# Gate logits from columns of the value blocks and from transposed normalised rows, and rows stored in four pieces, in a two-layer gated cross-attention kernel

## The reference

```python
x = x + tanh(g_xattn[0]) * L0_xattn(layernorm(x), ctx)
x = x + tanh(g_ffn[0]) * L0_ffn(layernorm(x))        # quantised gate/up/down
x = x + tanh(g_xattn[1]) * L1_xattn(layernorm(x), ctx)   # 16 heads, relative bias
x = x + tanh(g_ffn[1]) * L1_ffn(layernorm(x))        # 8 experts, the best one only
```

```python
x_red = x @ w_red                                    # 256 -> 16
logits = x_red @ (wg / norm(wg)).T                   # 16 -> 8
gates = softmax(logits); scores = max(gates); idx = argmax(gates)
h = gelu(x @ W1[idx] + b1[idx]); o = (h @ W2[idx] + b2[idx]) * scores
```

## Time and profile before

| | us |
|---|---|
| median of 3 runs | 456.87 (456.45 to 460.0) |
| profiled execution | 460.95 |
| its span, first to last instruction | 459.2 |
| TensorE busy | 405.7 (88%) |
| VectorE busy | 323.5 (70%) |
| ScalarE busy | 251.1 (55%) |
| POOL busy | 128.7 (28%) |
| mean granted TensorE clock | 0.958 |

### The profile page before, as it was taken

One profiled execution on the slowest core, in us unless ns is written; L12 is line 12 of the kernel. 1 busy time (PEld: TensorE's weight loads), 2 busy tenths in 40 slices (PEclk: granted clock), 3 DMA queues, 4 the chain that ended last, 5 costly groups with the idle time before them and its releaser, 6 DMA issues.

```text
span 459.2 us, 7477 instructions
## 1 busy us (share of the span) xinstructions
PE 405.7 (88%) x2436; PEld 289.4 (63%) x2437; DVE 323.5 (70%) x661; ACT 251.1 (55%) x420; POOL 128.7 (28%) x144
## 2 busy tenths in 40 slices
PE   7998899999996039999999999999958799999993
PEld 7877644444443038878877767876746476767762
DVE  4999984369998998964777898775473365555652
ACT  3564655579998965512487767777423323424210
POOL 6523155000000350421195000100126345351222
PEclk9999999999999558999999999999997899999998
DMA  8910000000001013000399000000092212121000
GB/s 244 287 5 0 1 3 0 0 0 0 0 1 61 1 38 73 1 0 0 127 396 390 7 1 2 0 1 2 10 267 77 64 55 66 52 60 33 27 21 1
DMA packets 27424, 27.25 MB, mean 59 GB/s; under 512 B 11611, under 2 KB 23586, under 8 KB 27139
## 3 DMA queue, kind: packets, MB, share of 16 engines
q1 hardware_dynamic: 25187, 21.73, 15.3%
q0 software_dynamic: 2208, 5.14, 3.9%
HBM read 22.63 MB, written 5.15 MB: 61 GB/s over the span
## 4 chain that ended last, share of the span: by engine, by line
PE 57%; DVE 21%; issue 4%; DMA 3%; ACT 2%; POOL 1%; DVEq 0%; POOLq 0%; ACTq 0%
PE quad L1668 24%; PE bank L1668 23%; PE bank L1961 4%; DVE amP L1371 3%; DVE big_g L1402 2%; PE bank L2156 2%; DMA token_rows<-x_rows 2%; DVE mx L1498 2%; DVE big_g L486 2%; DVE big_g L1499 2%; PE quad L1712 1%; DVE big_g L1496 1%; DVE amZ L1305 1%; DVE amU L1311 1%; PE bank L1712 1%
## 5 line engine op out<-in xcount | busy, mean ns | idle before, releaser
L1668 PE MATMUL quad<-yT,ffn_w 128*128 (+1 forms) x128 | 56.3, 593 | 0.0
L1668 PE MATMUL quad<-big_g,yT 128*128 x92 | 43.3, 613 | 3.5 <-issue 3.5
L769 ACT ACTIVATE big_u<-bank 77x512 f32<-77x512 f32 (+2 forms) x72 | 39.0, 593 | 11.2 <-PE bank L1961 10.4
L1067 ACT ACTIVATE yT<-yT 128x512 f32<-128x512 f32 x23 | 14.5, 630 | 53.0 <-DVE yT L1623 53.0
L1668 PEld LDWEIGHTS quad<-yT,ffn_w 128*128 128x128 f32 x128 | 24.0, 190 | 29.5 <-issue 28.3
L1668 PE MATMUL bank<-big_u,yT 128*128 x184 | 41.8, 380 | 0.2 <-DVE yT L1637 0.2
L746 POOL DMA_INDIRECT out<-yT,k_blockdiag x23 | 23.4, 1015 | 55.3 <-DVE yT L1637 48.4
L1668 PEld LDWEIGHTS bank<-big_u,yT 128*128 128x128 f32 x184 | 34.1, 190 | 5.0 <-issue 0.9
L1961 PE MATMUL bank<-ident,big_g 128*77 128x128 f32 x256 | 34.7, 278 | 1.2 <-ACT big_g L994 0.9
L1623 DVE TENSOR_TENSOR yT<-quad,ffn_w 128x512 f32<-128x512 f32 x23 | 15.9, 691 | 25.3 <-PE quad L1668 18.6
L1668 PE MATMUL quad<-ffn_w,big_u 128*128 128x256 f32 x144 | 31.6, 380 | 0.6 <-ACT big_u L769 0.6
(11 more groups left out here) (321 smaller groups left out, 913.5 us busy)
## 6 DMA issues: line engine op xcount, KB each, us to landing
big_g<-in_L_ffn_W SPq DMA_DIRECT2D x1, 4096.0 KB, 13.4
big_u<-in_L_ffn_W SPq DMA_DIRECT2D x1, 4096.0 KB, 24.9
x_rows<-in_x SPq DMA_DIRECT2D x4, 512.0 KB, 6.5
ffn_w<-in_L_ffn_b SPq DMA_DIRECT2D x1, 2048.0 KB, 26.8
tmp<-bias_by_distance SPq DMA_DIRECT2D x2, 616.0 KB, 6.8
token_rows<-x_rows SPq DMA_DIRECT2D x1, 1032.0 KB, 10.7
tmp<-in_L_ffn_b SPq DMA_DIRECT2D x1, 1024.0 KB, 6.4
token_rows<-x_rows SPq DMA_DIRECT2D x1, 774.0 KB, 11.9
```

The lines of the kernel that those rows point to most:

```text
L769: act.activation(out_, in_, ACT.Copy, **k).then_inc(done, 1)
L1067: act.activation(hb[:, u, :], hb[:, u, :], ACT.Gelu).then_inc(s.gelu_sb, 1)
L1668: return pe.matmul(out_, lhsT=lhsT, rhs=rhs, start=first, stop=last)
```

## The change

The logits of a finished row are those of the row before attention, plus those of the attended part and of the output bias. So they are now made in three parts, without the finished rows.

- Operand stage: the values transposed (`VT`), the output matrix transposed (`WOT`), `WOT` times `GM` (`WOB`, spread over the heads of a half), and from these 8 more columns for each head in the value block `V1`, where zeros were, with the bias of the output in the first head. `heads` is as large as before. TensorE does it in `layer1_operands` and `value_logits`, with 10 of the 14 idle products between its two steps.
- `head_out` divides the gate columns too, and `gate_sums` adds them over the heads into `LA`. `y3_logits` multiplies the transposed normalised rows by `GM` in the pairs 6 and 8; `y3_logits_back` returns them in the last pair; VectorE multiplies them by the deviation before attention (`stdp`, new on POOL) and adds `LA`.
- `y4_in`, `logits` and `logits_back` are gone, with ScalarE's copies for them.
- The last pair has its own order on TensorE, VectorE and ScalarE. `project` is now one call for each tile.
- The last two tiles' mean and variance come from a sum taken with the residual and from squares on ScalarE, after the one-hots.
- POOL writes the two extra columns of the rows. SyncE stores four pieces: tiles 0 to 7, 8 to 11, 12 and 13, 14 and 15, and loads `B2` after the first piece, once the logits are back.
- The weights' split is on VectorE after the index, the products of `SHARE` are after `inputs` of the second tiles.
- Two small loads (columns of the two biases) are new, and the near-bias loads wait for the gate columns (`VGS`).

(Indentation and blank lines are cut.)

```diff
 sp.wait_ge(s.kbd_sb, 1)
 sp.dma_start(B1, row(a["L1_ffn_b1"].rearrange("e h -> (e h)")).to_broadcast([P, E * HID])).then_inc(s.ld_b, 16)
-sp.wait_ge(s.x3_done, NT)
-sp.dma_start(B2, row(a["L1_ffn_b2"].rearrange("e h -> (e h)")).to_broadcast([P, E * D])).then_inc(s.ld_b, 16)
 rows_t = rows_d.rearrange("(t p) c -> p t c", p=P)
-sp.wait_ge(s.ln_row, 1)
-sp.dma_start(rows_t[:, 0:TB, :], X[:, 0:TB, :]).then_inc(s.row_stored, 16)
-sp.dma_start(rows_t[:, TB:LAST, :], X[:, TB:LAST, :]).then_inc(s.row_stored, 16)
-sp.wait_ge(s.ln_row, 2)
-sp.dma_start(rows_t[:, LAST:NT, :], X[:, LAST:NT, :]).then_inc(s.row_stored, 16)
+for n, (b, e) in enumerate(ROW_PARTS):
+    if n == 1:
+        sp.wait_ge(s.lg_ps, 1)
+        sp.dma_start(B2, row(a["L1_ffn_b2"].rearrange("e h -> (e h)")).to_broadcast([P, E * D])).then_inc(s.ld_b, 16)
+    sp.wait_ge(s.ln_row, n + 1)
+    sp.dma_start(rows_t[:, b:e, :], X[:, b:e, :]).then_inc(s.row_stored, 16)
...
-rstds_of(0, TB, s.mv_d, s.rstd_d, TB)
-rstds_of(TB, LAST, s.mv_d, s.rstd_d, LAST)
-pool.wait_ge(s.rstd_d, 2)
+def rows_ready(b, e, n):
+    pool.wait_ge(s.mv_d, n)
+    c.link(pool.tensor_scalar(ve4[:, b:e], mv4[:, b:e, 1], EPS, None, ALU.add))
+    c.link(pool.tensor_tensor(rstd4[:, b:e], ve4[:, b:e], mhalf[:, b:e], ALU.pow))
+    pool.tensor_copy(X[:, b:e, RSTD], rstd4[:, b:e])
+    c.link(pool.tensor_scalar(ve4[:, b:e], mv4[:, b:e, 0], -1.0, None, ALU.mult))
+    pool.tensor_tensor(X[:, b:e, NMR], ve4[:, b:e], rstd4[:, b:e], ALU.mult).then_inc(s.ln_row, 1)
+for b, e in ROW_PARTS[:-1]:
+    rows_ready(b, e, e)
...
+pool.tensor_scalar(nmean[:, :], xsum[:, :], -1.0 / D, None, ALU.mult).then_inc(s.nmean_sb, 1)
+pool.wait_ge(s.dev_sb, 2)
+c.link(pool.tensor_scalar(ve4[:, LAST:NT], xdev[:, :], 1.0 / D, EPS, ALU.mult, ALU.add))
+c.link(pool.tensor_tensor(rstd4[:, LAST:NT], ve4[:, LAST:NT], mhalf[:, LAST:NT], ALU.pow))
+pool.tensor_copy(X[:, LAST:NT, RSTD], rstd4[:, LAST:NT])
+pool.wait_ge(s.nmean_sb, 1)
+pool.tensor_tensor(X[:, LAST:NT, NMR], nmean[:, :], rstd4[:, LAST:NT], ALU.mult).then_inc(s.ln_row, 1)
 c.link(pool.tensor_copy(rstdp[:, LAST:NT], rstd4[:, LAST:NT]))
 pool.wait_ge(s.lx_sb, 1)
...
+copy(WOT, pb[3].rearrange("p (c n) -> p c n", c=CH), s.l1_ps, WOTS, s.woT_sb)
+copy(WGNT[:, :], pb[7][0:G, WOG_AT + CH * E:WOG_AT + CH * E + E], s.l1_ps, WGT_, s.wgT_sb)
 act.wait_ge(s.keepv_sb, 1)
 for b in range(NB):
     copy(V1[:, b * H:(b + 1) * H, 0:HD], pb[5][0:KEYS, b * D:(b + 1) * D].rearrange("p (n d) -> p n d", d=HD),
          s.l1_ps, V1S, s.v1_sb, scale=keepv[:, b:b + 1])
+copy(GM[:, :, 0:E], pb[7][:, 0:CH * E].rearrange("p (c e) -> p c e", c=CH), s.l1_ps, GMS, s.gm_sb)
+for ci in range(CH):
+    o = VT_AT + ci * NB * KEYS
+    act.activation(VT[:, ci, :], pb[7][:, o:o + NB * KEYS], ACT.Identity, bias=bv1c[:, ci:ci + 1]).then_inc(s.vT_sb, 1)
+for b in range(NB):
+    copy(V1[:, b * H:(b + 1) * H, HD + 1:HD + 1 + E],
+         pb[6][0:KEYS, D + b * H * E:D + (b + 1) * H * E].rearrange("p (n e) -> p n e", e=E),
+         s.l1_ps, VGS, s.v1_sb, scale=keepv[:, b:b + 1])
 def ints(o, n, k):
...
+        return
+    if t in NEAR_AT:
+        n = NEAR_AT.index(t)
+        copy(lT[:, 2 * n:2 * n + 2, :], pb[7][:, 0:2 * P].rearrange("p (b n) -> p b n", b=2),
+             s.lT_ps, 2 * n + 2, s.lT_sb)
     weightsT(t, 0, 0)
...
+weightsT(LAST, 0, 0)
+exponents(LAST, 1, 0)
+weightsT(LAST, 0, 1)
+exponents(LAST, 1, 1)
 weightsT(LAST, 1, 0)
+heads_out(LAST, 0)
 attended(LAST - 2)
 weightsT(LAST, 1, 1)
...
+act.wait_ge(s.nmean_sb, 1)
+act.wait_ge(s.x3_done, NT)
+for u in range(2):
+    act.activation(e_[:, u, 0:D], X[:, LAST + u, 0:D], ACT.Square, bias=nmean[:, u:u + 1],
+                   accum_out=xdev[:, u:u + 1]).then_inc(s.dev_sb, 1)
...
+dve.wait_ge(s.l1_ps, WOGS)
+dve.tensor_tensor(WOB, pb[7][:, WOG_AT:WOG_AT + CH * E].rearrange("p (c e) -> p c e", c=CH)
+                  .unsqueeze(2).to_broadcast([P, CH, 8, E]),
+                  headof[:, :].unsqueeze(1).unsqueeze(3).to_broadcast([P, CH, 8, E]),
+                  ALU.mult).then_inc(s.wob_sb, 1)
 dve.wait_ge(s.ar_sb, MP)
...
+    o = pb[5 + u][:, 0:H * VE].rearrange("p (h d) -> p h d", d=VE)
     c.link(dve.reciprocal(rd[:, u, :], o[:, :, HD]))
+    mark = c.mark(dve.tensor_tensor(GA[:, u, :, :], o[:, :, HD + 1:HD + 1 + E],
+                                    rd[:, u, :].unsqueeze(2).to_broadcast([P, H, E]), ALU.mult))
     dve.tensor_tensor(att[:, u, :].rearrange("p (h d) -> p h d", d=HD), o[:, :, 0:HD],
                       rd[:, u, :].unsqueeze(2).to_broadcast([P, H, HD]), ALU.mult).then_inc(s.att_sb, 1)
+    return mark
+def gate_sums(t, mark):
+    dve.wait_ge(s.dve_step, mark)
+    return dve.tensor_reduce(LA[:, t:t + 2, :], GA.rearrange("p u h e -> p u e h"), AX.X, ALU.add)
+def last_heads_out():
+    dve.wait_ge(s.o_ps, LAST + 2)
+    o = quad[:, 0:2, 0:H * VE].rearrange("p u (h d) -> p u h d", d=VE)
+    c.link(dve.reciprocal(rd[:, :, :], o[:, :, :, HD]))
+    mark = c.mark(dve.tensor_tensor(GA, o[:, :, :, HD + 1:HD + 1 + E],
+                                    rd[:, :, :].unsqueeze(3).to_broadcast([P, 2, H, E]), ALU.mult))
+    dve.tensor_tensor(att.rearrange("p u (h d) -> p u h d", d=HD), o[:, :, :, 0:HD],
+                      rd[:, :, :].unsqueeze(3).to_broadcast([P, 2, H, HD]), ALU.mult).then_inc(s.att_sb, 2)
+    c.link(gate_sums(LAST, mark))
 def residual(t, u):
-    dve.wait_ge(s.wo_ps, t + 2)
-    x = X[:, tile_at(t) + u, 0:D]
-    dve.tensor_tensor(x, pb[5 if t == LAST else 4][:, u * D:(u + 1) * D], x, ALU.add).then_inc(s.x3_done, 1)
+    dve.wait_ge(s.wo_ps, t + (u if t == LAST else 1) + 1)
+    x, ps = X[:, tile_at(t) + u, 0:D], pb[5 - u if t == LAST else 4][:, u * D:(u + 1) * D]
+    if t == LAST:
+        ins = dve.scalar_tensor_tensor(x, ps, 1.0, x, ALU.mult, ALU.add, accum_out=xsum[:, u:u + 1])
+    else:
+        ins = dve.tensor_tensor(x, ps, x, ALU.add)
+    ins.then_inc(s.x3_done, 1)
...
+    if 4 <= t < LAST:
         dve.wait_ge(s.bo_added, 1)
         residual(t - 4, 0)
         residual(t - 4, 1)
         moments(t - 4)
     unit(t, 1, 0)
-    head_out(t - 2, 0)
+    if t < LAST:
+        head_out(t - 2, 0)
     unit(t, 1, 1)
-    head_out(t - 2, 1)
+    if t == LAST:
+        head_out(t - 2, 0)
+    c.mark(gate_sums(t - 2, head_out(t - 2, 1)))
 first_pair()
 for t in range(2, NT, 2):
     pair(t)
+residual(LAST - 4, 0)
+residual(LAST - 4, 1)
+moments(LAST - 4)
+dve.wait_ge(s.std_sb, 1)
+dve.wait_ge(s.lg_ps, 1)
+c.link(dve.tensor_tensor(LOG.rearrange("p (u b) e -> p u b e", u=4),
+                         pb[2].rearrange("p (b u x) -> p u b x", b=4, u=4)[:, :, :, 0:E],
+                         stdp[:, :].rearrange("p (u b) -> p u b", u=4).unsqueeze(3).to_broadcast([P, 4, 4, E]),
+                         ALU.mult))
 residual(LAST - 2, 0)
 residual(LAST - 2, 1)
 moments(LAST - 2)
-def ln_rows(a, b):
...
-dve.wait_ge(s.lg_ps, NT // 4)
-lg = pb[1].rearrange("p (t e) -> p t e", e=32)[:, :, 0:E]
+last_heads_out()
...
 dve.wait_ge(s.cnt_ps, 1)
...
-dve.wait_ge(s.vals_sb, 1)
+dve.wait_ge(s.ex_sb, 1)
+c.link(dve.tensor_reduce(coef[:, :], EX, AX.X, ALU.add))
+c.link(dve.reciprocal(coef[:, :], coef[:, :]))
+c.link(dve.tensor_scalar(coef[:, :], coef[:, :], tg[:, 3:4], None, ALU.mult))
+c.link(dve.tensor_copy(vals[:, :, 2], coef[:, :]))
...
-step(0, (0, 1), ())
+for u in range(2):
+    bias1(u, 0)
+shares()
+for u in range(2):
+    hidden(u, 0)
...
-    pe.transpose(pb[6][0:G, D:D + E], wgn[:, :], ident[0:E, 0:E]).then_inc(s.l1_ps, 1)
+    pe.transpose(pb[7][0:G, WOG_AT + CH * E:WOG_AT + CH * E + E], wgn[:, :], ident[0:E, 0:E]).then_inc(s.l1_ps, 1)
     pe.wait_ge(s.wgT_sb, 1)
     for ci in range(CH):
         ins = mm(pb[7][:, ci * E:(ci + 1) * E], WRT[:, ci * P:(ci + 1) * P], WGNT[:, :], True, True)
     ins.then_inc(s.l1_ps, 1)
+def value_logits():
+    pe.wait_ge(s.gm_sb, 1)
+    pe.wait_ge(s.woT_sb, 1)
+    pe.wait_ge(s.vT_sb, CH)
+    for rj in range(CH):
+        for ci in range(CH):
+            ins = mm(pb[7][:, WOG_AT + rj * E:WOG_AT + (rj + 1) * E], WOT[:, ci, rj * P:(rj + 1) * P],
+                     GM[:, ci, 0:E], ci == 0, ci == CH - 1)
+    ins.then_inc(s.l1_ps, 1)
+    idle_work(pb[3], 10)
+    pe.wait_ge(s.wob_sb, 1)
+    for b in range(NB):
+        for ci in reversed(range(CH)):
+            o = D + (b * H + ci * 8) * E
+            mm(pb[6][0:KEYS, o:o + 8 * E], VT[:, ci, b * KEYS:(b + 1) * KEYS],
+               WOB[:, ci, :, :].rearrange("p h e -> p (h e)"), True, ci > 0)
+        o = D + b * H * E
+        for ci in range(CH):
+            ins = mm(pb[6][0:KEYS, o:o + E], bo1c[:, ci:ci + 1].to_broadcast([P, KEYS]), GM[:, ci, 0:E],
+                     False, ci == CH - 1)
...
 pe.wait_ge(s.wT_sb, 9)
+value_logits()
 pe.wait_ge(s.p_done, NQB + 1)
-idle_work(pb[3], 14)
+idle_work(pb[3], 4)
...
     ins.then_inc(s.oT_ps, 1)
+def y3_logits(b):
+    for ci in range(CH):
+        for u in range(4):
+            o = (4 * u + b) * P
```

(55 more changed lines are left out.)

227 lines of the change are left out of this document (86 added, 141 removed).

## The result

| | before | after |
|---|---|---|
| median of 14 runs, us | 457.55 (456.45 to 460.62) | 454.43 (451.6 to 456.05, and one disturbed execution of 501.6) |
| profiled execution, us | 460.95 | 452.23 |
| its span, us | 459.2 | 450.5 |
| mean granted TensorE clock | 0.958 | 0.96 |

The ratio is 0.9917, with a 95% interval of 0.9895 to 0.9939: 0.8% faster, which counts as within 1%. Two later comparisons of the same two kernels gave 0.9946 (0.9919 to 0.9972) and 0.9935 (0.9909 to 0.996). The median fell by 3.1, 2.2 and 3.2 us. The median after is that of all 14 executions; without the disturbed one it is 454.18. The two profiled spans differ by 8.7 us, and most of the experiments ask what lies between 8.7 and 3.

What follows compares the result with a forecast made beforehand. TensorE bounds most stages, VectorE pairs 6 and 8, the last store the first gather. Span 459.2 + 3.0 + 1.3 - 6.4 + 0.6 = 457.7 us, shifted to the runs' median: 455.4 us; 8-in-10 range 450.8 to 459.5.

Steps and rivals of the forecast that it cites:

- Operand stage, +3.0 predicted: Before the pairs: new products delay `down` to 179.5 and the next stage to 200.6; +3.0 us, bounds +2.0 to +4.8.
- Pairs, +1.3 predicted: Attention pairs: VectorE's additions and TensorE's `y3_logits` show in near-bias pairs 6 and 8; +1.3 us, between 0.6 and 2.2.
- Gate, -6.4 predicted: Last pair to first gather: earlier index and stores start the gather at 339.6, not 345.99; -6.4 us, bounds -7.5 and -4.5.
- a slow clock as a rival: Operand stage: TensorE stays at 1.2 GHz until `down` runs, 4.8 + 2 us there, time 459.2; chance 0.05.
- decides, but only by 1.0 us: End of the gate before the change: the last store releases the first gather; without it the gather would wait for the index.
- the last store still decides: Rival at the gather: last piece takes 9.2 us, gather starts at 344.3, gain only 1.7, time 460.1; chance 0.08.
- Share products, +0.6 predicted: After the gather: share products move behind `inputs`, 1.14 us of TensorE, hidden only if the 2.94 us stand remains; +0.6 us.
- The stand of 2.94 us: First expert steps before the change: TensorE stands 2.94 us before 359.54, then runs at half its clock; no row explains it.
- the stand goes: Rival in the first expert steps: the 2.94 us stand and slow clock vanish, saving 4.7 us, time 451.2; chance 0.13.
- 453 to 458.5: The forecast's own range in us, from adding the bounds of the terms.
- signs named for "right": After-profile: `down` 3 to 4 us later, pairs 6 and 8 1 to 2 more, one-hots 5.7 earlier, gather 2.1 earlier, awaiting index.
- sign of "wrong": After-profile: gather released by `token_rows<-x_rows`; `down` before 177.5; pair without near bias over 12.35 us; bias waiting for share product.

Runs made afterwards that it cites:

- before_again: The kernel before, unchanged, profiled and timed again: median 457.03 us over 22 runs, profiled span 454.8 us.
- after_again: The changed kernel, unchanged, profiled and timed a second time: median 454.86 us over 10 runs, ratio to before 0.9946, profiled span 455.8 us.
- pair_sums_out: The changed kernel without VectorE's gate products and sums in pairs 0 to 12 (zeros instead): median 454.3 us over 10 runs.
- before_b2_early: The kernel before with one wait changed, so that B2 loads when the twelfth tile's rows are finished: one execution, 456.92 us.
- stores_undone: The changed kernel with the old transfer order, B2 loaded after the last residual and rows stored at the third and fourth signals: median 460.49 us.
- gate_columns_out: The changed kernel without the operands of the gate columns (zeros instead) and with 14 idle products as before: median 453.16 us over 7 runs.

## Why the prediction was right

Forecast 455.4, measured 454.4, 454.9 and 454.8; range 450.8 to 459.5; the chance of 0.72 was on within 1%. The call was right, and so was the main line of the mechanism: a gain of about 6 us in the gate, of which the stages ahead take a part back. That the sum came within 1 us is partly luck. The stages ahead were charged 4.3 us and take 1.8 to 2.8; against that, the half clock takes up to 1.5 us of the forecast gain in the gate and up to 2.8 us in layer 1 in some executions, and these were in no term of the sum. The profiles divide as follows, against before_again.

**Operand stage, +3.0 predicted: +1.0 or +2.0 at fill(0, 0), 1.7 in the time.** The order of the work came as predicted: idle products until 176.2, gate columns after, `down` at 178.5 to 179.5 with 179.5 forecast. Two sizes were off. The 16 records of the gate columns took 1.06 us with the clock up (176.18 to 177.25), 0.066 each, where I had taken 0.12 and 1.9 in all; they took 1.9 at the half clock in after_again, and 1.1 to 1.6 in the four other profiles with the late clock, which rose while they ran. And of the 3.4 us by which `down` starts later in after_again, 0.9 is gone at y3_in, mostly the wait for VectorE that TensorE no longer has, which was in the prediction, and another 0.6 at fill(0, 0), which was not; that VectorE, not delayed as much, is the bound of the second four tiles would explain it, but no run takes it apart.

**Pairs, +1.3 predicted: +0.8.** fill(6, 0) to fill(14, 0) is 52.3 us in all three profiles of the changed kernel, 51.5 before. It is VectorE's work as predicted, and pair_sums_out takes exactly this away. The step that failed is that TensorE's logits were charged ahead of `fill(8, 1)`, at 1.3 us a pair and 2.6 in the two: the 32 records of a pair took 1.06 us, and pair_sums_out, which keeps them and is back at the 13.44 us of before, shows that even those lie under VectorE.

**Gate, -6.4 predicted: -6.6 with the clock up, -4.9 to -5.1 with it down.** From fill(14, 0) to the gather: 39.67 us before, 33.08, 34.60 and 34.77 after. Counted from fill(14, 0), the one-hots are ready 0.6 us, the totals start 0.9 and the index is written 0.8 us earlier than forecast (340.37 less the 1.94 us by which fill(14, 0) is later is 338.4, for 339.25), since `token_back` came 0.7 earlier. What I did not see is written in the rows above: the new order lets TensorE stand 0.72, 1.51 and 0.75 us in a row. The waits were in my sum, their effect on the clock was not. I priced a slow clock as a rival only ahead of `down`.

**The store that "decides, but only by 1.0 us" was a misreading.** The gather starts 0.30 us after a store lands, but 0.93 us after VectorE has written the index (340.37 to 341.30). In the kernel before these two came out at 345.99 and 345.93: a tie. before_b2_early shows it. I took 0.3 for both. The 0.6 us that this lacks at the new start were covered by the path, which was 0.8 us shorter than I had it; that the gain in the gate came out so near is luck to this extent. Both edits were needed, the shorter path and the stores out of its way: with the stores undone the changed kernel is slower than the one before, 1.0053 (1.0021 to 1.0084), and with B2 early the kernel before gains nothing. The rival "the last store still decides" gave 460.1, and the kernel with the stores undone measured 460.5. The start of its gather agrees too (348.6 by the rival, 348.65), but the two sums are made of other pieces: 3.0 us were lost ahead of fill(14, 0) for 4.3, the gate gained 0.5 for 1.7, and behind the gather 2.5 were lost for 0.6 (111.15 against 108.67). It was rightly held unlikely for this one: the last piece took 2.8 us. The Trainium skill, SBUF — State Buffer, section The DMA setup-cost knee, gave an estimated 2.6, and the trace agrees (2.8).

**Share products, +0.6 predicted: +0.5 (109.2 against 108.7 us from gather to end), if the clock holds.** The share products used to fill the time ahead of the first rows, with 12 idle products around them. The change kept the 12 and took the share products away from there, so TensorE stands 1.2 us more, and in single executions layer 1 starts at the half clock: 6.52 us for 3.70 in one of the three profiles of the changed kernel, and 4.95 in gate_columns_out, whose end is the same (the 5.82 of stores_undone come behind its own longer stand). This cost was in no term.

**The stand of 2.94 us** was in the profile of before only. I gave "the stand goes" 0.13 as an effect of the change; it was no effect of the change. That the sum was made against the profiled execution and then shifted to the median (4.1 us) kept it out of the forecast: luck, since nothing in the prediction said that the shift was mostly this stand. The 8.7 us between the first two profiles are 4.4 us of this stand and its slow clock, and 4.3 that the change gives in the best case: -6.6 in the gate, +0.8 in the pairs, +1.0 ahead of them, +0.5 behind. The two other profiles of the changed kernel, with half clocks, are 1.6 us under before_again (453.2 against 454.8) and 1.0 over it (455.8). The medians lie between, at 2.2 to 3.2 under. What makes a single execution keep or lose the clock was not found.

**The range and the signs.** The bounds of the terms add up to 452.6 to 460.0, not to the "453 to 458.5" of the prediction; the wider range for 8 in 10 does not hang on it. Of the signs named for "right", `down` came 2.6 to 3.7 us later, and the gather waited for its index. Its start was 4.7 us earlier than 345.99 in the first profile, and 2.2 and 2.0 in the others, for 2.1. The pairs 6 and 8 took only 0.7 us more together (27.53 against 26.87 from fill(6, 0) to fill(10, 0)), for 1 to 2. The one-hots of the first profile came 7.4 us earlier against fill(14, 0); the 5.7 in the list is what the prediction had worked out for the totals. One sign of "wrong" did show: fill(10, 0) to fill(12, 0), a pair without near bias, took 12.46 us for 12.31 before, over the 12.35 that were named. In pair_sums_out it is 12.31 again, so here too VectorE's additions showed where they were held to be free, at 0.15 us.

## What to carry to other kernels

When a change takes waits off the path, list the breaks that it gives TensorE and not only their sum: a break ahead of dense products costs its length and then, in some executions, half speed in what follows, and a few idle products in it can give that back (taking twelve away cost 2.9 us here). Take a second profile of the unchanged kernel before you price a wait that no row explains. Where two releasers of one instruction are compared, compare them with their own lags: a store's landing and an index's writing were 0.3 and 0.9 us away from the gather.

## What the runs showed of the hardware

- Behind the three breaks of 0.72, 1.51 and 0.75 us the granted clock fell to its lower level (1.2 GHz) in two of the three profiles of the changed kernel and stayed at 2.4 GHz in the third. In all three kernels profiled with idle products in these breaks it stayed up. The Trainium skill, TensorE: Matmul & The Clock Gate, section Why this matters for your kernels, warns of longer idle gaps between bursts of products. The runs agree that idle gaps cost the clock, but show it behind a row of gaps of at most 1.51 us, which its rule would let pass.
- An indirect gather on POOL began 0.93, 0.94 and 0.93 us after VectorE's write of its index, and 0.30 us after the landing of a store that it waited for.
- 258 KB took 2.8 us alone, 3.5 us when 1.8 MB had been issued 8 us ahead of them, and 9.2 to 10.4 us behind 2.8 MB issued within 5 us.
- VectorE's sum of 256 elements with a stride took 0.60 to 0.62 us, where I had taken 0.42 from a product of the same size.
- Products with 8 columns cost 0.23 us a record at 1.2 GHz with the weights changed each time, those of the gate columns 0.066 at 2.4 GHz.
